# Two of eight gated fusions moved from the four row banks into the cross attention's bank, beside the first mixture attention; weights awaited in three parts

## The reference, cut to what matters

```python
# layer 0, the fusion
memory_proj = jnp.einsum('bme,de->bmd', memory, W_mem)
scores = jnp.einsum('bnd,bmd->bnm', hidden_states, memory_proj) / jnp.sqrt(jnp.float32(D))
attn = jax.nn.softmax(scores, axis=-1)
memory_context = jnp.einsum('bnm,bmd->bnd', attn, memory_proj)
gate_input = jnp.concatenate([hidden_states, memory_context], axis=-1)
gate = jax.nn.sigmoid(jnp.einsum('bnf,df->bnd', gate_input, W_gate) + b_gate)
fused = hidden_states + gate * memory_context
return _rmsnorm(fused, norm_w)
...
# layers 1 and 3, the mixture
x = rms_norm(hidden_states, ln_in_w)
mixed = jnp.where(vm, x @ v_qkv, x @ l_qkv)
q, k, v = jnp.split(mixed, 3, axis=-1)
...
ctx = sdpa(q, k, v, causal=True)
attn_out = jnp.where(vm, ctx @ v_dense, ctx @ l_dense)
hidden_states = residual + attn_out
ci = rms_norm(hidden_states, ln_post_cross_w)
```

## Time and profile before

| | before |
|---|---|
| median of 3 runs | 1388.88 us |
| lowest and highest | 1388.78, 1389.87 us |
| the profiled execution | 1388.42 us, of which the span from first to last instruction is 1386.5 us |
| PE busy in the span | 1314.9 us (95%) |
| DVE, ACT, POOL busy | 764.6, 473.6, 451.3 us |
| mean granted clock of PE | 0.98 |

### The profile page before, as it was taken

How to read it: one execution, slowest core, us unless ns; L and a number is a source line. 1 busy time by engine, 2 the same in 40 slices (tenths; PEclk the granted TensorE clock), 3 DMA queues, 4 the chain that set the end, 5 groups by cost and what they waited for, 6 DMA issues and landing times.

```text
span 1386.5 us, 26030 instructions
## 1 busy us (share of the span) xinstructions
PE 1314.9 (95%) x10995; PEld 1055.5 (76%) x10995; DVE 764.6 (55%) x1361; ACT 473.6 (34%) x785; POOL 451.3 (33%) x558
## 2 busy tenths in 40 slices
PE   7977899999999999999999999989899999999988
PEld 5755677787886777888888888876678787787766
DVE  4455575666666656353344434445667566666553
ACT  3323333423324223244345443433332333313321
POOL 1143444444344332211111111324334344334332
PEclk9978999999999999999999999999999999999999
DMA  9010000000001001200000000011000000000000
GB/s 324 7 61 1 2 2 2 1 2 1 2 6 42 2 20 39 86 17 1 1 0 1 0 1 0 1 41 42 2 2 2 1 17 1 2 16 2 1 17 17
DMA packets 19903, 27.31 MB, mean 20 GB/s; under 512 B 3433, under 2 KB 15553, under 8 KB 19521
## 3 DMA queue, kind: packets, MB, share of 16 engines
q1 hardware_dynamic: 19008, 24.20, 5.2%
q10 hardware_dynamic: 768, 1.26, 0.3%
HBM read 23.35 MB, written 2.10 MB: 18 GB/s over the span
## 4 chain that ended last, share of the span: by engine, by line
PE 84%; DVE 6%; ACT 4%; POOL 3%; issue 2%; DMA 0%; SPq 0%; ACTq 0%; DVEq 0%; POOLq 0%
PE bank L1418 6%; PE bank L1708 6%; PE bank L1673 5%; PE bank L1678 5%; PE bank L1562 5%; PE bank L1914 4%; PE bank L1878 4%; PE bank L1921 4%; PE row_banks L1512 4%; PE row_banks L1822 3%; PE row_banks L1545 3%; PE bank L1480 3%; PE bank L1697 3%; PE bank L1411 3%; PE row_banks L1517 2%; ACT room L2032 2%
## 5 line engine op out<-in xcount | busy, mean ns | idle before, releaser
L1269 POOL TENSOR_SCALAR_AFFINE_SELECT room<-room 128x1024 f32<-128x1024 f32 x64 | 70.7, 1108 | 186.4 <-ACT room L2032 186.4
L2274 DVE TENSOR_REDUCE room<-row_banks 128x4 f32<-128x512 f32 (+1 forms) x128 | 116.4, 952 | 23.4 <-PE row_banks L1517 23.0
L2032 ACT ACTIVATE room<-row_banks 128x1536 f32<-128x1536 f32 x64 | 92.9, 1451 | 89.6 <-PE row_banks L1545 89.6
L1708 PE MATMUL bank<-room,down_w 128*128 128x256 f32 x384 | 94.4, 386 | 0.5 <-DVE room L2374 0.5
L2288 DVE RECIPROCAL room<-bank 128x256 f32<-128x256 f32 x32 | 56.1, 1754 | 59.3 <-PE bank L1562 59.3
L2064 ACT ACTIVATE room<-bank 128x256 f32<-128x256 f32 x96 | 36.4, 383 | 147.7 <-PE bank L1678 136.7
L1231 POOL TENSOR_TENSOR room<-room 128x256 f32<-128x256 f32 x32 | 24.5, 766 | 171.8 <-ACT room L2044 171.8
L1708 PEld LDWEIGHTS bank<-room,down_w 128*128 128x128 f32 x384 | 69.6, 190 | 13.6 <-issue 4.9
L1342 POOL TENSOR_TENSOR room<-room 128x512 f32<-128x512 f32 x32 | 33.7, 1070 | 133.1 <-DVE room L2474 132.9
L1545 PE MATMUL row_banks<-room 32*128 32x256 f32 (+1 forms) x1024 | 62.1, 357 | 9.7 <-ACT room L2032 4.6
L1545 PEld LDWEIGHTS row_banks<-room 32*128 32x128 f32 x1024 | 48.9, 191 | 27.6 <-issue 15.6
(11 more groups left out here) (242 smaller groups left out, 3037.8 us busy)
## 6 DMA issues: line engine op xcount, KB each, us to landing
out_x<-wq SPq DMA_DIRECT2D x8, 256.0 KB, 2.3
qkv<-in_L_xattn_v_qkv SPq DMA_DIRECT2D x2, 768.0 KB, 6.4
qkv<-in_L_xattn_l_qkv SPq DMA_DIRECT2D x2, 768.0 KB, 9.2
gate_w<-in_L_xattn_v_gate SPq DMA_DIRECT2D x2, 640.0 KB, 8.4
gate_w<-in_L_xattn_l_gate SPq DMA_DIRECT2D x2, 640.0 KB, 7.6
up_w<-in_L_xattn_v_up SPq DMA_DIRECT2D x2, 640.0 KB, 6.2
up_w<-in_L_xattn_l_up SPq DMA_DIRECT2D x2, 640.0 KB, 6.5
down_w<-in_L_xattn_v_down SPq DMA_DIRECT2D x2, 640.0 KB, 6.4
```

The lines of the kernel that those rows point to most:

```text
L1269: pool.affine_select(out=diagonal, in_=diagonal, compare_op=ALU.is_ge, fill=0.0, base=0, pattern=[[0, 8], [1, P]], channel_multiplier=-1)\
L1708: return pe.matmul(ff_bank[0][:, t * S:(t + 1) * S], down_w[:, f, t * P:(t + 1) * P], hid[:, i, :], start=(i == t == 0), stop=(i == UPS - ...
L2032: act.activation(probs[w % 2], row_banks[:, :, 0:3 * P], ACT.Exp).then_inc(*ATT_ACT.does(e, f"exp{w}"))
L2274: last = dve.tensor_reduce(dst, row_banks[:, :, P * i:P + S * i], X, ALU.max, negate=True)
```

## The change

Three things are done.

Examples 6 and 7 are fused in `crs_bank` instead of the row banks, one after the other. With that `first_scores 0 0` waits for the fusion of example 5 alone, `memory 0` (the first user of `crs_bank`) waits for that of example 7, and the tables put the stages of both among the first stages of the mixture layer. They still take buffer sets 2 and 3.

```diff
+F_ROWS = 6
...
         def f_bank(e):
-            return row_banks[:, e % FS, :]
+            return row_banks[:, e % FS, :] if e < F_ROWS else crs_bank[:]
...
                         if e == 0:
-                            pe.wait_ge(*F_DVE.did(B - 1, "y"))
+                            pe.wait_ge(*F_DVE.did(F_ROWS - 1, "y"))
...
                 def memory(e):
+                    if e % B == 0:
+                        pe.wait_ge(attn_in, 16 * ATTN_DMAS * (e // B + 1))
                     if e == 0:
-                        pe.wait_ge(*X_ACT.did(B - 1, "x"))
+                        pe.wait_ge(*F_DVE.did(B - 1, "y"))
...
                 def f_scores(e):
-                    if e >= FS:
+                    if e == F_ROWS:
+                        pe.wait_ge(*X_ACT.did(B - 1, "x"))
+                    if e > F_ROWS:
+                        pe.wait_ge(*F_DVE.did(e - 1, "y"))
+                    elif e >= FS:
                         pe.wait_ge(*F_DVE.did(e - FS, "y"))
```

```diff
                     if e % B == 0:
-                        pe.wait_ge(mot_in, 16 * MOT_DMAS * (e // B + 1))
+                        pe.wait_ge(qkv_in, 16 * QKV_DMAS * (e // B + 1))
...
+                load_attention(sp, mot_w[0])
                 sp.wait_ge(pads_zero, 3)
-                load_mot(sp, mot_w[0])
                 load_mot_ff(sp, mot_w[0])
```

And all the tables have new numbers, so that the order differs in many other places too. Two lines show the kind:

```diff
-    put(-9564.6366, "f_add")
...
+    put(-10522.5682, "f_add")
```

More of the change, by code:

```diff
@@ L204, in fuse_stages @@
[L204 to L206 removed]
+    put(-10522.5682, "f_add")
+    put(-10522.0171, "f_rstd")
+    put(-818.3939, "f_shift")
+    put(-818.1199, "f_sums")
+    put(-811.0101, "f_gated")
+    put(-809.8928, "f_mean")
+    put(-809.3953, "f_y")
+    put(-458.5001, "f_exp")
+    put(-457.9064, "f_turn_out")
+    put(-457.5212, "f_context_out")
+    put(-455.5781, "f_tanh")
+    put(-455.0273, "f_square")
+    put(1621.9773, "f_scores")
+    put(1622.6213, "f_turn")
@@ new lines, in fuse_stages, with fuse_sixth_stages, put @@
+    put(1622.9973, "f_context")
+    put(1623.5427, "f_gate")
+    put(1630.5315, "f_sum")
+    put(1630.9407, "f_spread")
+    return at
+def fuse_sixth_stages():
+    at = []
+    def put(time, stage, *which):
+        at.append((time, stage, *which))
+    put(1853.0372, "f_add")
+    put(1868.4458, "f_rstd")
+    put(2232.1757, "f_shift")
+    put(2234.9403, "f_sums")
+    put(2592.6191, "f_exp")
+    put(2594.9236, "f_turn_out")
+    put(2648.9041, "f_gated")
+    put(2654.4959, "f_mean")
+    put(2656.3415, "f_y")
+    put(3046.3464, "f_context_out")
+    put(3047.3478, "f_tanh")
+    put(3048.7212, "f_square")
+    put(4672.5135, "f_scores")
+    put(4680.1964, "f_turn")
+    put(4680.5971, "f_context")
+    put(4696.2914, "f_gate")
+    put(4716.4206, "f_sum")
+    put(4717.1028, "f_spread")
+    return at
@@ new lines, in fuse_last_stages, with put @@
+def fuse_last_stages():
+    at = []
+    def put(time, stage, *which):
+        at.append((time, stage, *which))
+    put(1917.4378, "f_add")
+    put(1924.9166, "f_rstd")
+    put(2666.8145, "f_shift")
+    put(2670.0968, "f_sums")
+    put(2690.6004, "f_gated")
+    put(2712.4370, "f_mean")
+    put(2721.1042, "f_y")
+    put(3079.0554, "f_exp")
+    put(3082.4619, "f_turn_out")
+    put(3100.5269, "f_context_out")
+    put(3104.8157, "f_tanh")
+    put(3118.4478, "f_square")
+    put(4707.0493, "f_scores")
+    put(4734.0984, "f_turn")
+    put(4749.9688, "f_context")
+    put(4753.0174, "f_gate")
+    put(4777.3431, "f_sum")
+    put(4781.2084, "f_spread")
@@ L951, in each @@
     def each(starts, stages, first=0):
-        for e in range(B):
-            order.extend((starts[e] + time, stage, first + e, *which) for time, stage, *which in stages)
+        for e, start in enumerate(starts):
+            order.extend((start + time, stage, first + e, *which) for time, stage, *which in stages)
     def by_parity(starts, stages_of, layer):
```

1283 lines of the change are left out of this document (638 added, 645 removed).

## The result

The changed kernel took 1405.46 us (median of 4 runs, 1403.18 to 1406.25) against 1389.38 for before in the same session: a ratio of 1.0116, 95% interval 1.0102 to 1.0130. The forecast was 1387.6 with a range of 1380.5 to 1393.5, and "slower" had 0.25; the measured time is 12 us above the range. The profiled execution is 1405.11 us, its span 1403.1, the mean granted clock 0.967 against 0.980.

A forecast was written before the change was run, and what follows sets the result against it. PE was taken as the bound, busy 1314.9 of 1386.5 us. Terms -0.6 - 1.5 - 1.0 + 1.8 = -1.3 against the profiled 1388.42 gave 1387.1; with 0.46 for the median of runs, 1387.6 us, range 1380.5 to 1393.5.

The forecast's parts named there:

- The weights: Splitting the weight semaphore and issuing the third layer's loads later removes no wait: cost 0.
- The waits of the start: PE idle time at the start, over stretches A, B, C and D: -0.6 us in sum.
- A: From the last gate ahead of the norm to `q 0`: idle 4.0 us against 5.9, -1.9.
- B: From `v 0` to `q 1`: idle 5.2 us against 3.1, +2.1.
- C: Last of the first scores to the second scores of example 0: idle 4.4 us against 7.0, -2.6.
- D: Behind `dense 0`, which loses its cover `k 2` and `v 2`: idle 2.9 us against 1.1, +1.8.
- The clock: Matmul time at the low clock in A, B and C: -1.5 us, bounds -8.6 to +3.
- the bound "+3": Upper bound of the clock term: a fall in each of A to C with a gate's 3.6 us doubled twice.
- rival 2: Slower: D grows thin, the clock falls before `cross_first 0`, 4.5 us of work at half speed: +4.5, 1392.1; chance 0.25.
- sum of 8.6: Low-clock cost before the change, in us: A 4.0, B 1.7, C 2.9; the most the clock could give back.
- Rival 1: Gates keep the clock up in at least two of A, B, C: clock term -6, 1383.1 us; chance 0.29.
- The other places: Full stretches 0, end of layer 1 -1.0, 890 to 1040 us +1.8, the up tile at the end 0.

The follow-up runs named there:

- e1: The kernel before with the change's three weight semaphores and load issue places alone, order and banks kept; 1389.41 us, ratio 0.9993.
- e13: e9 with each of its 40 added matmuls replaced by two of one column in the same places; 1394.65 us, ratio 1.0045.
- e14: e9 with each of its 40 added matmuls replaced by two of 64 columns; 1385.56 us, ratio 0.9977.
- e12: The change with eleven added matmuls nobody reads in the waits behind memory 15, dense 15 and crs_sum 15 0; 1400.13 us, ratio 1.0087.
- e9: The kernel before with 40 added matmuls of 256 columns that nobody reads, in the waits of the start; 1379.98 us, ratio 0.9942.
- e5: The change with eight added matmuls of 256 columns between the fusion's sums and spreads, ahead of 44.7 us; 1397.43 us, ratio 1.0057.
- e4: The change with the fusions of examples 0 to 3 run together again as before; 1402.86 us, ratio 1.0080.
- e17: e9 with 20 more such matmuls in the waits of 901 to 1004 us; 1377.51 us, ratio 0.9914.
- e15: The change's banks, with fusions of examples 0 to 5, half of 6, and all behind the start in the old order; 1394.32 us, ratio 1.0045.

## Why the prediction was wrong, step by step

**The weights, 0:** right (e1).

**The waits of the start, -0.6:** right in kind. They fell more: by 5.6 us in the windows. Stretch by stretch, idle time before, forecast, and measured (the sum of the waits in brackets of its timeline):

| | before | forecast | after |
|---|---|---|---|
| A, last gate to `q 0` | 5.9 | 4.0 | 2.8 |
| B, `v 0` to `q 1` | 3.1 | 5.2 | 4.1 |
| C, through the second scores of example 0 | 7.0 | 4.4 | 3.0 |
| D, behind `dense 0` | 1.1 | 2.9 | 1.9 |

The releasers are the named ones: no wait at `q 0`, waits at `crs_sum 0` and `cross_q 0`, none at `memory 0`, no transfer. `n0_spread 1` stands 4.2 us behind `v 0` (forecast 4.4), `q 1` 8.3 (7.85). B and D in after:

```profile
93.98 0.61 PE L1488 MATMUL bank<-mean_w,room 128*128 128x1 f32 x4 [1.43 <-POOL room L1288]
96.27 1.12 PE L1493 MATMUL bank<-const,room 128*128 128x128 f32 x4 [1.69 <-POOL room L1385]
97.93 1.97 PE L1822 MATMUL bank<-room,x_all 128*128 128x64 f32 x8 [0.54 <-DVE x_all L2485]
100.35 3.75 PE L1479 MATMUL bank<-room,qkv 128*128 128x256 f32 x8 [0.46 <-DVE room L2299]
...
159.14 0.61 PE L1488 MATMUL bank<-mean_w,room 128*128 128x1 f32 x4 [0.69 <-POOL room L1292]
...
163.44 2.07 PE L1663 MATMUL bank<-room,cq_w 128*128 128x256 f32 x4 [0.96 <-DVE room L2293]
...
171.01 1.66 PE L1606 MATMUL row_banks<-room 32*128 32x256 f32 x16 [2.56 <-DVE room L2350]
```

**The clock, -1.5:** this is the step that failed, in size and in sign. It measured about +13.6 in the start and +5.3 behind it, by half. The argument was that each fall costs what it cost before, and that gates behind a thin stretch lift the clock. That came out in A alone: with `f_gate 6` there, the low stretch has 5.3 us of busy time instead of 8.8, 1.7 us less by half. The clock was below full four times before 140 us, not three. Three things were wrong. First, the bound "+3" assumed that falls can only repeat where PE idled; the fusion's own rows at 40 to 58 us, which I took for work that merely moves at its old duration, fell too (6.8 us by half of its busy time). Nor does the bound follow from its own terms: a gate's 3.6 us doubled twice is 7.2. Second, moving work into a thin stretch puts that work at the low clock: B now holds `q 1`, `k 1` and scores for 12.3 us of busy time at 0.50 where before it was 3.4, and C 8.9 where it was 6.4. Filling an idle stretch with sums and scores of few columns left the clock down and made the bill larger. Third, rival 2 named the fall in D for 4.5 us. It came (160.7 to 167.6) and a second behind it (171.0 to 177.8), 5.5 us by half against 2.6 in the one of before. That one, at 163.1 to 169.9 us, was missing from the prediction's sum of 8.6, which has A, B and C alone. Rival 2's mechanism was right, as one of several, and its condition too: the clock fell ahead of `cross_first 0`. Rival 1 wanted the clock to stay up in two of A, B and C; it fell in all three.

The Trainium skill, in "TensorE: Matmul & The Clock Gate", section "HAM oscillation — how this bites in real kernels", speaks of bursts of matmuls that are shorter than the waits between them, each of which starts cold. The trace is of that kind in B (a sum of 0.61 us between waits of 1.43 and 1.69) and behind D (0.66 us of `turn_max 1` ahead of a wait of 2.56). From 44.7 to 58.3 us it is not: the waits ahead of the fall were 1.0 us in all and PE was then busy 13.57 of 13.65 us. e13 and e14 show low stretches with a full queue too.

**The other places, +0.8:** measured +7.7 behind the start by the windows, of which +1.6 is idle time and +5.3 half of the busy time at the low clock. Of the forecast's two terms, the -1.0 around the end of layer 1 measured +0.3 (idle 5.7 us from 507 to 578 against 5.5 from 495 to 565) and the +1.8 behind it +0.2 (13.2 us from 903 to 1055 against 13.0 from 890 to 1040). "At the end one up tile changes its place: 0" was the second step to fail. Before, `up 14 0` stood between `dense 15` and `crs_sum 15 0` and covered the square and the add (first two rows, before); now nothing does (the other rows, after):

```profile
1324.89 1.99 PE L1418 MATMUL bank<-room,dense 128*128 128x256 f32 x8 [1.46 <-DVE room L2303]
...
1329.97 0.60 PE L1427 MATMUL bank<-mean_w,room 128*128 128x1 f32 x4 [0.47 <-POOL room L1231]
...
1337.24 2.76 PE L1479 MATMUL bank<-room,dense 128*128 128x256 f32 x8 [2.13 <-DVE room L2372]
1339.79 1.80 PE L1472 MATMUL bank<-room,dense 128*128 128x64 f32 x8
1343.84 1.01 PE L1488 MATMUL bank<-mean_w,room 128*128 128x1 f32 x4 [2.25 <-POOL room L1292]
1345.89 0.69 PE L1493 MATMUL bank<-const,room 128*128 128x128 f32 x2 [1.04 <-POOL room L1374]
```

The waits alone are given back later (PE idles 12 us in the last 70 us of after and in the last 66 of before). The low clock is not: 5.0 us by half of 10.09, and e12 got 4.3 to 5.3 back. The fall itself, at 1338.3 us, comes behind the longer wait ahead of `dense 15` and ahead of the uncovered one; e12 filled both, so which of them it takes is open.

**The sum.** Idle -4.0 and work +20.6 make the 16.6 us between the two spans. The forecast had idle -0.6 (with -1.0 and +1.8 beside it, +0.2 in all) and work -1.5.

## What to carry to other kernels

When PE is the bound, count two things where an order changes: its waits, and what its matmuls weigh in columns. Here sums of one column, transposes and scores of 64 columns counted as busy and ran at the low clock in a full queue (e13, e14 and 44.7 to 58.3 us of after), where wide matmuls of the same busy time kept it up (e9). So spread them between wide matmuls, above all behind a wait, and be wary of filling one with them. A few wide matmuls into a free bank, no more than fit into the wait, are a cheap test of what the clock costs (1.0% here), and here also the gain. Read the granted clock of every stretch that a change touches, full ones too.

## What was not expected of the hardware

A matmul stream that is busy 99% ran at 0.50 of the clock: 13.57 of 13.65 us in after, where all but one context and the gate at its end had 1 to 128 columns, and 13.35 of 13.65 in e13, where sums and one-column fills lead up to `q 0`. The same short matmuls without a wait and behind wide ones ran at 1.00 (e5, 47.0 to 52.4 us). Whether a marginal stretch falls differs between runs of one kernel: e4 had 1397.85 at a mean clock of 0.975 beside 1403.7 at 0.968, and in before three of 16 runs were at 1394 to 1397 with 0.974 to 0.977 where the others had 0.980 or 0.981. The profiled run of e17 was its slowest, 1384.65, with such a fall at 49 to 66 us that its other four runs, by their clock of 0.997 to 0.999, did not have. What exactly decides a marginal stretch stays open: e4 and e15, whose banks are the same, show only that the order of the stages there matters.
